# Attention with keys loaded by feature, four narrow pieces of peaks for each head, and another order of the work on all engines

## The reference, cut to what matters

```python
gi = concatenate([q, k, v], -1)
ig = (gi @ igate_w.T + igate_b).transpose(0, 2, 1)
fg = (gi @ fgate_w.T + fgate_b).transpose(0, 2, 1)
cs = cumsum(log_sigmoid(fg), -1)
log_D = where(tril, cs[..., :, None] - cs[..., None, :], -inf) + ig[..., None, :]
max_log_D = max(log_D, -1, keepdims=True)
D = exp(log_D - max_log_D)
C = (qh @ kh.T / sqrt(dh)) * D
normalizer = maximum(abs(C.sum(-1, keepdims=True)), exp(-max_log_D))
h = (C / (normalizer + EPS)) @ vh            # then a norm over each head
Sm = softmax(xf @ Wr + br)                   # the router, of the second norm's rows
```

## Time and profile before

| | |
|---|---|
| median of 3 runs | 3057.1 us (3056.25 to 3057.47) |
| profiled execution, span | 3051.6 us |
| around the span (3057.1 - 3051.6) | 5.5 us |
| PE busy, of the span | 2948.7 us (97%) |
| DVE, ACT, POOL busy | 1819.7, 1132.8, 1065.5 us |
| DMA | 250.71 MB, mean 82 GB/s |

### The profile page before, as it was taken

How to read it: one execution, slowest core, us unless ns; L and a number is a source line. 1 busy time by engine, 2 the same in 40 slices (tenths; PEclk the granted TensorE clock), 3 DMA queues, 4 the chain that set the end, 5 groups by cost and what they waited for, 6 DMA issues and landing times.

```text
span 3051.6 us, 60802 instructions
## 1 busy us (share of the span) xinstructions
PE 2948.7 (97%) x24708; PEld 2395.3 (78%) x24708; DVE 1819.7 (60%) x5124; ACT 1132.8 (37%) x2025; POOL 1065.5 (35%) x1029
## 2 busy tenths in 40 slices
PE   6999999999997599999999999999999999999998
PEld 5888888888886477777777877787787787778886
DVE  6999999999998645354454444444434445444332
ACT  5788788787886211121121121122112122112110
POOL 4777777777776311111122111121112112121111
PEclk9999999999998699999999999999999999999999
DMA  3243444434443412241242132232123214222121
GB/s 122 100 160 120 162 139 149 161 123 165 141 134 113 131 40 37 35 99 31 46 99 48 36 80 35 37 96 62 31 38 93 41 31 111 38 50 57 35 37 24
DMA packets 140575, 250.71 MB, mean 82 GB/s; under 512 B 31968, under 2 KB 31968, under 8 KB 140296
## 3 DMA queue, kind: packets, MB, share of 16 engines
q1 hardware_dynamic: 106296, 170.80, 17.2%
q0 software_dynamic: 28672, 67.65, 12.6%
q10 hardware_dynamic: 5328, 8.36, 0.9%
HBM read 137.23 MB, written 101.19 MB: 78 GB/s over the span
## 4 chain that ended last, share of the span: by engine, by line
PE 64%; DVE 1%; DMA 1%; issue 0%; ACT 0%; POOL 0%; ACTq 0%; DVEq 0%; POOLq 0%
PE DN L1729 32%; PE UP L1700 30%; PE TT L1673 1%; DMA w_raw<-in_L_ffn_W_down 1%; DVE c_hit L1392 0%; PE c_bank L1385 0%; DVE down_lo L1258 0%; PE c_bank L1369 0%; DVE c_hit L1413 0%; ACT z L1643 0%; DVE c_within L1408 0%; ACT down_hi L1252 0%; POOL out_x L1618 0%; DVE c_gained L1445 0%; DVE mid_lo L1761 0%
## 5 line engine op out<-in xcount | busy, mean ns | idle before, releaser
L1618 POOL DMA_INDIRECT out_x<-y,slots x128 | 208.5, 1629 | 1621.1 <-DVE y L1785 1621.1
L1643 ACT ACTIVATE z<-UP,bup 128x512 f32<-128x512 f32 (+1 forms) x352 | 240.8, 686 | 1085.6 <-PE UP L1700 1066.5
L1729 PE MATMUL DN<-down_hi,mid_hi 128*128 128x512 f32 x1408 | 570.8, 405 | 0.0
L1700 PE MATMUL UP<-xT_hi,up_lo 128*128 128x512 f32 (+1 forms) x1408 | 555.5, 395 | 0.0
L1700 PE MATMUL UP<-xT_hi,up_hi 128*128 128x512 f32 (+1 forms) x1408 | 553.5, 393 | 1.8 <-DVE xT_lo L1740 0.9
L1700 PE MATMUL UP<-xT_lo,up_hi 128*128 128x512 f32 (+1 forms) x1408 | 552.0, 392 | 0.0
L1729 PE MATMUL DN<-down_hi,mid_lo 128*128 128x512 f32 x1280 | 505.8, 395 | 0.0
L1729 PE MATMUL DN<-down_lo,mid_hi 128*128 128x512 f32 x1280 | 505.7, 395 | 0.0
L1759 DVE CAST mid_hi<-z 128x512 fp32r<-128x512 f32 (+1 forms) x352 | 151.2, 429 | 486.4 <-ACT z L1643 486.4
L1783 DVE TENSOR_TENSOR y<-DN,bdn 128x512 f32<-128x512 f32 x128 | 88.5, 692 | 432.3 <-PE DN L1729 419.5
L1700 PEld LDWEIGHTS UP<-xT_hi,up_hi 128*128 128x128 f32 (+1 forms) x1408 | 260.3, 185 | 67.5 <-ACT z L1643 2.8
(11 more groups left out here) (264 smaller groups left out, 4971.9 us busy)
## 6 DMA issues: line engine op xcount, KB each, us to landing
xs<-in_x SPq DMA_DIRECT2D x64, 512.0 KB, 3.7
kraw<-in_ctx SPq DMA_DIRECT2D x32, 1024.0 KB, 7.3
out_x<-xs SPq DMA_DIRECT2D x32, 1024.0 KB, 12.5
rows_scratch<-xfb SPq DMA_DIRECT2D x32, 1024.0 KB, 10.6
w_raw<-in_L_ffn_W_down SPq DMA_DIRECT2D x40, 512.0 KB, 4.4
w_raw<-in_L_ffn_W_up SPq DMA_DIRECT2D x16, 682.5 KB, 4.1
mid_hi<-mid_hi ACTq DMA_DIRECT2D x32, 86.0 KB
mid_lo<-mid_hi ACTq DMA_DIRECT2D x32, 84.0 KB
```

What stands on the lines that cost most here:

```text
L1618: pool.indirect_dma_start(out_rows, bass.IndirectOffsetOnAxis(ap=slots[:, m:m + 1], axis=0), y[:, t, :], None, compute_op=ALU.add).then_in ...
L1643: act.activation(z[0:r, k % 2, :], UP[k % 3][0:r, :], ACT.Silu, bias=bup[0:r, e // 2, f:f + 1]).then_inc(s["z"], 1)
L1700: mm = pe.matmul(UP[k % 3][0:r, :], weights.up[wa][:, c, f * P:f * P + r], xT[xa][:, c, :], start=first, stop=(c == CH - 1 and wa == 1))
L1729: mm = pe.matmul(DN[m % 2][:, :], lhs, rhs, start=first, stop=(f == FCH - 1 and lhs is parts[-1][0]))
```

## The change

- Keys: the host gives the context a second time, by feature. `load_keys` loads it into kT in two halves for each batch; the turns of K on PE and their copies on ACT go. The context by rows (kraw) is still loaded, for v.
- Decays: climb first, then peaks, masks last. peaks and inner hold 128 columns; the tile is chosen by selectors with zero rows (sel, selP have a form for each tile or side). Peaks take 8 pieces of 128 columns (before 4 of 256), widths 3 of 128 (before 1 of 384). DVE makes peaks in one operation and not 4, inner in one and not 3.
- DVE multiplies both heads of a pair at once (1024 wide), sums squares of two pairs at once, and makes the router's softmax for 4 batches at once (GROUP).
- All 8 banks are shared by the plan, which now lists pairs too; scores stand behind products.
- The order on every engine is written anew.

```diff
-            plan = [("qw", b2, 0, "dve", 0), ("q", b1, 0, "act", 1), ("k", b1, 0, "act", 2), ("q", b1, 1, "act", 3), ("k", b1, 1, "act", 1),
...
+            plan = [("product", b3, 3, None), ("scores", b2, 1, None), ("decays", b2, 1, None),
+                    ("q", b1, 0, 6), ("q", b1, 1, 7), ("q", b1, 2, 0), ("q", b1, 3, 1), ("qw", b2, 1, 4),
+                    ("st", b2, 0, 5), ("st", b2, 1, 2), ("st", b2, 2, 3), ("gates", b1, 0, 0),
+                    ("xfT", b5, 0, 1), ("xfT", b5, 1, 5), ("xfT", b5, 2, 4), ("xfT", b5, 3, 2), ("lt", b6, 0, 3), ("shift", b1, 0, 0),
+                    ("product", b2, 0, None), ("scores", b2, 2, None), ("decays", b2, 2, None), ("ends", b1, 0, 0), ("qw", b2, 2, 1),
...
+                def load_keys(b, half):
+                    c = slice(half * CH // 2, (half + 1) * CH // 2)
+                    if b >= 2:
+                        sp.wait_ge(s["qk"], PAIRS * (b - 2) + (half + 1) * PAIRS // 2)
+                    sp.dma_start(kT[:, b % 2, c, :], k_v[b][:, c, :]).then_inc(s_kt[half][b % 2], 16)
...
                         turned_rows(b5, 2)
...
                     if live(b1):
                         chunk_totals(b1)
                     if live(b2):
-                        decay_factors(b2, 3)
+                        numerators(b2, 0)
+                        squares(b2, 0)
+                    rsqrt_guess(i)
+                    if live(b5):
+                        turned_rows(b5, 3)
+                    if live(b2):
+                        decay_factors(b2, 2)
...
                 def scores(b, p):
...
+                    wait_cleared(pe, "scores", b, p)
...
                 def decays(b, p):
...
-                    for a, r, mask in ((0, top, (maskneg, maskswap)), (1, end, (maskswap, maskneg))):
-                        for t, m in zip((top, end), mask):
-                            pe.matmul(EX[t, a, :], identb[r, r], m[r, :], start=True, stop=False, skip_group_check=True)
...
                     for par in range(2):
+                        for n in range(2):
+                            for a, r in ((0, top), (1, end)):
+                                at = (2 * par + n) * P
+                                pe.matmul(EX[:, a, at:at + P], sel[r, n, 2 * p + par, :], peaks[r, b % 2, :],
+                                          start=False, stop=False, skip_group_check=True)
+                    for t, swap in ((top, 0), (end, 1)):
                         for a, r in ((0, top), (1, end)):
...
+                            m = (maskneg, maskswap)[(a + swap) % 2]
+                            mm = pe.matmul(EX[t, a, :], identb[r, r], spread(m[r, :], 1, TILES), start=False, stop=True, skip_group_check=True)
...
                 def widths(b, p):
...
+                    for j in range(1, TILES):
+                        mm = pe.matmul(t[:, (j - 1) * P:j * P], selP[:, j - 1, 2 * p:2 * p + 2, :].rearrange("k a d -> k (a d)"), inner[:, b % 2, :],
+                                       start=True, stop=True)
...
                     if live(b2):
-                        decays(b2, 3)
-                        widths(b2, 3)
+                        product(b2, 0)
+                        scores(b2, 2)
+                        decays(b2, 2)
                     if live(b1):
                         chunk_ends(b1)
                     if live(b2):
+                        widths(b2, 2)
+
+                        product(b2, 1)
                         scores(b2, 3)
+                        decays(b2, 3)
+                        widths(b2, 3)
...
-                    for par in range(2):
-                        c = C[:, 2 * (g % CRING) + par, :]
...
+                    c = C[:, 2 * (g % CRING):2 * (g % CRING) + 2, :]
```

More of the change, by code:

```diff
@@ L154, in attention @@
         s_cd = [sem(f"a_cd{i}") for i in range(VBUF)]
+        s_kt = [[sem(f"a_kt{half}{i}") for i in range(2)] for half in range(2)]
         def live(b):
             return 0 <= b < NB
+        taken = {"q": "tq", "qw": "tqw", "xfT": "txf", "lt": "tlt", "shift": "tsh", "ends": "nm", "lg": "tlg", "turn": "ttu", "gates": "gs"}
+        PAIR_BANKS = {"scores": ("cc", (2, 3)), "decays": ("dd", (4, 5)), "product": ("an", (6, 7))}
         def iteration_fills(i):
-            b1, b2, b5, b6 = i - 1, i - 2, i - 5, i - 6
@@ L163, in iteration_fills @@
-            plan = [("qw", b2, 0, "dve", 0), ("q", b1, 0, "act", 1), ("k", b1, 0, "act", 2), ("q", b1, 1, "act", 3), ("k", b1, 1, "act", 1),
[L164 to L169, removed]
+            b1, b2, b3, b5, b6 = i - 1, i - 2, i - 3, i - 5, i - 6
@@ L170, in iteration_fills @@
             if i >= NB + 2:
[L171 to L174, removed]
+                plan = [("product", b3, 3, None), ("lt", b6, 0, 5)] if i == NB + 2 else []
+                plan += [("xfT", b5, c, c) for c in range(CH)]
@@ L179, in attention @@
         for i in range(NB + 5):
[L180 to L184, removed]
+            for kind, b, k, side in iteration_fills(i):
+                if kind in PAIR_BANKS:
+                    done, sides = PAIR_BANKS[kind]
+                    cleared[kind, b, k] = []
+                    for n in sides:
+                        if n in latest and latest[n] not in cleared[kind, b, k]:
+                            cleared[kind, b, k].append(latest[n])
+                        latest[n] = (s[done], PAIRS * b + k + 1)
@@ L896, in _ @@
                 ins.then_inc(s["clear"], 1)
[L897 to L898 removed]
+                step(dve.memset(gW[:, :, :], 0.0))
                 step(dve.memset(vv[:, :], 1.0))
@@ L1082, in gate_peaks @@
-                    for j in range(TILES):
-                        rows = slice(QD * j, QD * j + QD)
-                        ins = dve.scalar_tensor_tensor(out=peaks[rows, b % 2, j * P:(j + 1) * P], in0=run[rows, :], scalar=incoming[rows, :],
-                                                       in1=held[rows, 0, :].bitcast(FP32), op0=ALU.max, op1=ALU.subtract)
-                    ins.then_inc(s["xm"], 1)
+                        dve.wait_ge(s["inn"], b)
+                    step(dve.tensor_scalar(held[:, :], run[:, :], incoming, lows[:, 0:1], ALU.max, ALU.mult))
```

564 lines of the change are left out of this document (273 added, 291 removed).

## The result

The changed kernel takes 3229.4 us (3228.5 to 3237.3, 4 runs) where the kernel before takes 3057.3 us: a ratio of 1.0575, 95% interval [1.0558, 1.0591]. It is slower by 172 us. The forecast was 3169, slower by 112; the range (3092 to 3240) holds the time.

A forecast was written before the change was run, and what follows sets the result against it. PE was taken as the bound (busy 901.27 of 920 us). Terms −14.7, −12.1, +67.9 and +70.5 us sum to +111.6; with the profiled 3051.6 and 5.5 for the median this gives about 3169 us, range 3092 to 3240.

The forecast's parts named there:

- Work on PE: On PE, per batch: K's turns go (−1.76 us), peaks add 0.86 and widths 0.44; −14.7 us over 32 batches.
- Rival C: On PE the narrow pieces of peaks and widths run twice each: +104 us, 3273 us; chance 0.08.
- rival D: On PE the narrow pieces cost their columns alone, so peaks and widths add nothing: 3056 us; chance 0.09.
- The wait that goes: On PE, pair 1's scores move ahead of the chunk states and no longer wait for DVE: −12.1 us.
- The wait that comes: PE's scores(b2,2) wait for ACT's late fourth copy of turned rows: 2.34 us in 29 iterations, +67.9 us.
- The clock: Behind the new wait PE runs at half clock through the widths: +2.43 us in 29 iterations, +70.5 us.
- Case A: The forecast itself: PE's new wait comes and the clock falls to half behind it, 3169 us; chance 0.62.
- B: PE's new wait comes but the clock holds: 3098 us; chance 0.21.
- The upper bound given: For the half clock on PE: 6.8 us each time, if it stays down as long as at the start.
- What costs nothing: ACT's dropped copies, DVE's joined operations and the extra key loads stay hidden under PE's busy time: 0 us.

The follow-up runs named there:

- x4: Kernel before with only the keys loaded by feature, no turns of K on PE and no copies of K on ACT: 3047.9 us, ratio 0.9980.
- x6: Changed kernel with POOL's centred_values behind split_climb and POOL's two passes over the heads' output left out, ACT's copy of turned rows still late: 3193.9 us.
- x62: x6 plus 20 extra turns of the identity on PE behind product(b2,0), filling the wait: 3076.3 us.
- x61: x6 plus ACT's fourth copy of turned rows moved ahead of the first pair's numerators: 3015.9 us.
- z1: Kernel before with the running maximum of the gates in SBUF in place of PSUM (wt shares a buffer with low): 3244.7 us, ratio 1.0616.
- x3: Changed kernel with POOL's centred_values moved behind split_climb, so POOL is idle during DVE's head_variances: 3241.5 us.
- x7: Changed kernel with all its work, ACT's fourth copy of turned rows early, POOL's passes put between DVE's chains by waits: 3059.2 us, ratio 1.0013.
- x2: Changed kernel with 36 extra turns of the identity on PE behind product(b2,0), in the wait: 3193.4 us.

## Why the prediction was right, and where it was not

**Work on PE: right.** Peaks +0.16 and widths +0.20 for a pair at full clock (0.215 and 0.11 forecast), together +1.44 for a batch where 1.30 was forecast. Rival C (twice) and rival D (columns alone) are both out: 0.49 us for the peaks lies between 0.33 and 1.09, nearest to the 0.545 of the scores' row.

**The wait that goes: half right.** The waits for chunk states went; 15.6 us of other waits, most for DVE's C, came to the same line (139.1 − 123.5, the page). That term should have been near 0. Nor is work taken from PE worth its length: x4 took 56 us of it and gained 6.

**The wait that comes: right by itself.** 2.34 us were forecast, 2.44 measured where nothing else disturbs it (x6), and about 60 us of time (x62 against x61) for 67.9.

**The clock: right in kind, the term too small.** Case A, not B: the clock falls behind the wait. The term stood at 70.5 us; x6 against x62 gives about 118, with x6's 27 us of uncertainty. It was taken as if half clock ended with the widths (2.43 us lost is 4.86 us at half clock, where x6 has 8.7), as it about does at 507 us; in other iterations it goes on past the fourth pair's scores (0.50 from 575 to 577 us, back at 583). The upper bound given, 6.8 us each time, holds it (118/29 is 4.1).

**The step that failed: "What costs nothing", where DVE was put under PE's busy time.** It said "DVE joins its narrow operations; both were already under PE's busy time, so this gives nothing". Joined operations did get fewer, but their operand had moved from PSUM to SBUF, and that was taken as free; in z1 that place alone costs 189 us. Passed over too was when POOL works: lines 996 to 998, ahead of the row variances, now run beside `centred_values` and take 0.58 + 0.97 + 0.96 = 2.50 us, where before they took 0.61. The forecast did say that the wait would grow if DVE were late, and gave that no price. It grew by 2.11 us an iteration, 1.9 of it from these three lines (x3 shows it gone with them). This term was missing; 35 us of the result (3229 − 3194) come from it on top of the late copy, and 190 without the late copy.

So the forecast of slower, by the late copy and the clock, is borne out: with two of POOL's passes out, that cause alone brings 3194. Put in this order, the runs make the sum: −41 (x61 against before, 9 of it POOL's passes; forecast −27), +60 for the wait (68), +118 for the clock (71), +35 for DVE's meeting with POOL (0), together +172. The range held this because its upper end left room for the clock, not because the meeting was foreseen. In another order the terms come out otherwise, because PE and DVE wait for each other in one ring.

**What held DVE up.** The operations named, with their inputs in SBUF, take 0.6 to 1.3 us in the mean while POOL works, 0.2 to 0.4 when it doesn't, or when one input is in PSUM. POOL's own instructions are as long (after, 130 to 900 us):

```profile
L252 POOL TENSOR_TENSOR nsb<-nsb,Wo 128x512 f32<-128x512 f32 x88 | 102.8, 1200 | 1.7
...
L245 POOL TENSOR_TENSOR nsb<-nsb,rr 128x512 f32<-128x512 f32 x88 | 88.9, 1042 | 8.8 <-DVE nn L1012 8.8
```

That DVE waits for the POOL instruction in flight is shown by single instructions of this trace: all 22 of line 997 start while one runs and end 47 to 50 ns behind its end. Of line 1114, the 16 that start so take 1.19 to 1.22 us and end 82 to 88 ns behind it, and the 6 that do not take 0.33. In the kernel before, with run in PSUM, 80 of 104 peaks start with over 0.25 us of a POOL instruction left, and none takes more than 0.36. Not every operation on SBUF is held up: line 935 (BATCH_NORM_STATS2 of xs) takes 0.68 us either way. The trace names no port. The Trainium skill ("SBUF — State Buffer", section "SBUF: two separate sides") has the rule: VectorE and GpSimd share one pair of SBUF ports as an exclusive lock for a whole instruction, which a VectorE operation needs if it has two SBUF inputs or runs in a two-port mode, and then the other "fully blocks". The trace agrees, 0.210 against 0.967 us for line 997, and the forecast should have read it, for it spoke against this change.

Still open: why half clock lasts until 507 us in one iteration and past 581 in another; the runs show both, and don't tell what decides.

## What to carry to other kernels

When a buffer moves from PSUM to SBUF, look at who reads it on VectorE and what GpSimd does at that moment: a small operation can last as long as GpSimd's whole instruction (0.21 us became 0.97 here), and moving GpSimd's work may only move the meeting (x3). In a hand-written order, follow each wait back through every engine until it meets itself; in a ring, undoing one of two causes may show little (23 or 35 of 213 us here), so undo both and then one at a time. And price the second engine before counting a gain on the first: 56 us taken from TensorE were worth 6, since VectorE stood right behind it.

## What the runs showed of the hardware that was not expected

Behind a wait of 2.44 us in a TensorE stream otherwise without gaps the clock falls to half in 22 of 23 iterations (x6, 130 to 900 us; behind the one that ends at 539.75 it holds), and even behind waits of 1.5 us it does so in some (x7, mean clock 0.96). The Trainium skill ("TensorE: Matmul & The Clock Gate", section "Why this matters for your kernels") asks only to avoid longer gaps than these; here the measurement decides. Filling the wait with turns of no use made x6 faster by about 118 us (x62), and the changed kernel with all its work by 36 (x2): work that nobody needs was cheaper than the wait.
